# First layer of a four-layer image kernel: window rows in another order, copies of the inner rows, 25 rounds of products a group where there were 27

## What is computed

```python
def _denoise_block(x, w1, b1, w2, b2, w3, b3, a, b, c):
    trip = _triplets(x)             # channels t-1, t, t+1 (mirrored at the ends)
    xf = trip.reshape(B * T, C, H, W)
    o = a * _conv_reflect(xf, w1, b1, 1, 2) + b * _conv_reflect(xf, w2, b2, 2, 4) + c * _conv_reflect(xf, w3, b3, 4, 8)
    return jnp.tanh(o).reshape(B, T, H, W)
y = _denoise_block(x, blk1...)
z = _denoise_block(y, blk2...)
```

## Time and profile before

| | us |
|---|---|
| median of 3 runs | 5376.93 (5367.36 to 5379.23) |
| profiled execution, first to last instruction (the span) | 5383.9 |
| PE busy | 4994.9 (93% of the span) |
| DVE, ACT, POOL busy | 3365.2, 2396.6, 1362.4 |
| matmuls of the first layer's convolutions (L679) | 3027.2 busy, 55296 instructions |

### The profile page before, as it was taken

The page is one execution under the profiler, slowest core; times in us unless marked ns, Lnnn a source line. Parts: engine busy times, 40 slices in busy tenths (PEclk is TensorE's granted clock), DMA queues, the critical chain, the costliest instruction groups (busy, mean ns, idle before and its releaser), DMA issues. The chain is left out here.

```text
span 5383.9 us, 178367 instructions
## 1 busy us (share of the span) xinstructions
PE 4994.9 (93%) x78653; PEld 3092.8 (57%) x78653; DVE 3365.2 (63%) x6195; ACT 2396.6 (45%) x2999; POOL 1362.4 (25%) x1629
## 2 busy tenths in 40 slices
PE   4998999899899999999999997998777799999998
PEld 2444444444447569997666663443556466666665
DVE  5543444344342555555555546887999788888888
ACT  1222222222221111111111117885999689899997
POOL 0000000000001111111111100000777355555556
PEclk9999999999999999999999998999999999999999
DMA  8677777777666767667667657998688366666664
GB/s 246 217 228 235 224 228 232 223 223 237 222 209 199 226 200 239 207 203 236 203 208 236 205 178 277 321 325 302 256 308 309 129 152 152 150 150 153 151 152 120
DMA packets 366864, 1166.78 MB, mean 217 GB/s; under 512 B 60457, under 2 KB 61096, under 8 KB 287018
## 3 DMA queue, kind: packets, MB, share of 16 engines
q1 hardware_dynamic: 363928, 1152.98, 69.0%
q10 hardware_dynamic: 2162, 2.39, 0.2%
HBM read 683.58 MB, written 453.51 MB: 211 GB/s over the span
## 5 line engine op out<-in xcount | busy, mean ns | idle before, releaser
L679 PE MATMUL c_p<-c_w,wc 128*32 128x512 f16 x55296 | 3027.2, 381 | 91.1 <-DMA c_w<-xs 81.1
L679 PEld LDWEIGHTS c_p<-c_w,wc 128*32 128x32 f16 x55296 | 1896.0, 97 | 1194.4 <-DMA c_w<-xs 76.2
L739 ACT ACTIVATE c_t<-c_p,cbias,cscale 128x512 f32<-128x512 f32 x512 | 397.9, 777 | 2582.6 <-PE c_p L679 2582.6
L591 DVE TENSOR_SCALAR c_y<-c_t 128x512 f16<-128x512 f32 x256 | 109.2, 426 | 855.1 <-ACT c_t L739 854.1
L601 DVE TENSOR_TENSOR a_x<-c_t,a_x 128x512 f32<-128x512 f32 x256 | 221.3, 865 | 666.7 <-ACT c_t L739 658.5
L1699 PE MATMUL f_P<-f_qh,f_wt 64*64 64x512 f16 x4608 | 545.7, 378 | 1.8 <-DVE f_t L1595 1.8
L1699 PE MATMUL f_P<-f_hl,f_wt 64*64 64x512 f16 x4608 | 545.3, 379 | 0.0
L1860 POOL TENSOR_TENSOR f_y<-f_y,f_x 128x512 f32<-128x512 f32 x256 | 330.7, 1292 | 449.3 <-DVE f_hl L1574 443.2
L1595 DVE SCALAR_TENSOR_TENSOR f_t<-f_P,f_kk,f_ci 128x256 f32<-128x256 f32 x1024 | 423.4, 476 | 12.8 <-PE f_P L1699 7.6
L810 POOL COPY c_y<-c_y 128x16 f16<-128x16 f16 x512 | 85.6, 197 | 1360.7 <-DVE c_y L593 1360.7
L1459 POOL TENSOR_TENSOR e_hl<-e_g,e_hl 128x2048 f16<-128x2048 f32 x63 | 257.1, 4081 | 609.3 <-ACT e_hl L1409 609.3
(11 more groups left out here) (263 smaller groups left out, 5887.4 us busy)
## 6 DMA issues: line engine op xcount, KB each, us to landing
c_w<-xs SPq DMA_DIRECT2D x576, 264.0 KB, 5.6
c_w<-ys SPq DMA_DIRECT2D x576, 264.0 KB, 4.0
d_x<-x SPq DMA_DIRECT2D x128, 1024.0 KB, 7.6
x<-d_x SPq DMA_DIRECT2D x128, 1024.0 KB, 5.1
ys<-c_y SPq DMA_DIRECT2D x576, 132.0 KB
xs<-a_hl SPq DMA_DIRECT2D x70, 1056.0 KB, 9.8
a_x<-in_x SPq DMA_DIRECT2D x256, 256.0 KB, 6.8
a_x<-in_x SPq DMA_DIRECT2D x128, 512.0 KB, 5.2
```

The costliest lines, as they stand in the source:

```text
L679: t = p.matmul(pg[32 * j:32 * j + 32, :], wu[:, blk, wl, var, di, :], buf[:, bk, xl * PW + PAD + dx:xl * PW + PAD + dx + NW], start=(di == ...
L739: s.activation(tt_[n % 3][:, :], pp[:, n % 4, :], ACT.Tanh, bias=cbias[:, blk:blk + 1], scale=cscale[:, blk:blk + 1]).then_inc(c_act, 1)
```

## The change

The 32 rows of a window are put on the partitions in another order (`slot`): the 16 rows of the band first, then the 4 above and the 8 below, then the 4 farthest above. `load` follows it with four transfers for every two channels, of 32, 16, 8 and 8 partitions, where there were two of 32; the bytes are the same, and so are the 8448 bytes a partition. All semaphore counts of loads double.

Two small tensors with two buffers each are filled for every group by copies: `near` takes the high half of partitions 0 to 95 (the band's rows and 4 on each side; POOL, 96x2112 values) and, on partitions 96 to 127, the low half of partitions 64 to 95 (DVE, 32x2112); `twice` takes the low half of partitions 0 to 63 as it is (DVE, 64x2112) and, on partitions 64 to 127, the same shifted by 3 columns (ACT, 64x2052). With it the column offsets -2 and 1, and -1 and 2, are done by one product. `products` then has 15 rounds on the window for the offsets 0, -8, -4, 4, 8 as before, 4 of the low weights on the window, 4 on `near` and 2 on `twice`: 25.

The copies for group n + 1 stand on each of the three engines at the beginning of the loop's body for group n, ahead of the normalization steps, of the tables, of `halves`, `total` and `evict`. They wait for the loads of the group's unit and until group n - 1 is multiplied. PE waits for them inside the group, after 19 rounds (`near`) and after 23 (`twice`). POOL makes the weights for the six new products once, by 12 small copies ahead of the first group; the swapped copy of the weights grows from 432 to 576 KB a transfer and waits for them.

```diff
@@ -39,9 +39,8 @@
...
-        h8, s = ((1, 0), (0, 0), (1, 1), (0, 1))[row // 8 + 1]
-        v8 = row + 8 * h8 - 16 * s
-        return 8 * (2 * v8 + chan % 2) + 4 * s + 2 * h8 + chan // 2
+        place = row if 0 <= row < 16 else 16 + (row + 4 if -4 <= row < 0 else row - 12 if row >= 16 else row + 20)
+        return 4 * place + 2 * (chan % 2) + chan // 2
@@ -294,7 +293,9 @@
...
         h = sb(ctx, "a_hl", [128, 8, 2, PW], F16)
-        wc = [sb(ctx, f"wc{i}", [128, 2, 2, 3, 9, 32], F16) for i in range(2)]
+        wall = [sb(ctx, f"wc{i}", [128, 4608], F16) for i in range(2)]
+        wc = [w[:, 0:3456].rearrange("p (a b v d c) -> p a b v d c", a=2, b=2, v=3, d=9) for w in wall]
+        wn = [w[:, 3456:4608].rearrange("p (a v e c) -> p a v e c", a=2, v=3, e=6) for w in wall]
@@ -331,6 +332,8 @@
...
         win.append(sb(ctx, "c_w1", [128, 16, RW], F16))
+        near = [sb(ctx, f"c_n{i}", [128, 4, PW], F16) for i in range(2)]
+        twice = [sb(ctx, f"c_2{i}", [128, 4, PW], F16) for i in range(2)]
@@ -344,7 +347,8 @@
...
-        w_c, w_f, w_t, w_sel, w_hi = (sem("w_" + n) for n in ("c", "f", "t", "sel", "hi"))
+        w_c, w_f, w_t, w_sel, w_hi, w_wn = (sem("w_" + n) for n in ("c", "f", "t", "sel", "hi", "wn"))
+        c_nh, c_nl, c_2a, c_2b = (sem("c_" + n) for n in ("nh", "nl", "2a", "2b"))
@@ -378,7 +382,18 @@
...
-            return 128 * sum(1 + (place(r)[2] == 0) for r in range(u % 2, u + 1, 2) if r)
+            return 256 * sum(1 + (place(r)[2] == 0) for r in range(u % 2, u + 1, 2) if r)
+        def rows_in(e, n):
+            u, g = divmod(n, 4)
+            if u == 0:
+                e.wait_ge(c_l0[g // 2], 256)
+            elif g == 0:
+                e.wait_ge(c_ld[u % 2], n_win(u))
+            if n >= 2:
+                e.wait_ge(c_pe, n - 1)
+            return win[u % 2][:, 4 * g:4 * g + 4]
@@ -616,6 +631,11 @@
...
+                def copies(n):
+                    w = rows_in(v, n)
+                    v.tensor_copy(near[n % 2][96:128], w[64:96, :, PW:RW]).then_inc(c_nl, 1)
+                    v.tensor_copy(twice[n % 2][0:64], w[0:64, :, PW:RW]).then_inc(c_2a, 1)
@@ -629,10 +649,13 @@
...
                 v0(2), v1(2)
+                copies(0)
...
                         i, s = stage_of(u, g)
+                        if 4 * u + g + 1 < 8 * NU:
+                            copies(4 * u + g + 1)
@@ -664,22 +687,38 @@
...
                     if u == 0:
-                        p.wait_ge(c_l0[g // 2], 128)
+                        p.wait_ge(c_l0[g // 2], 256)
...
                         p.wait_ge(c_act, n - 3)
-                    for di, dx in enumerate(DX):
-                        for z, (wl, xl) in enumerate(((0, 0), (0, 1), (1, 0))):
-                            for j in range(4):
-                                bk = 4 * g + j
-                                var = 0 if (half, bk) == (0, 0) else (2 if (half, bk) == (1, 15) else 1)
-                                t = p.matmul(
-                                    pg[32 * j:32 * j + 32, :], wu[:, blk, wl, var, di, :],
-                                    buf[:, bk, xl * PW + PAD + dx:xl * PW + PAD + dx + NW],
-                                    start=(di == 0 and z == 0), stop=(di == 8 and z == 2), tile_position=(0, 32 * j))
+                    def four(weights, source, at, start=False, stop=False):
+                        for j in range(4):
+                            bk = 4 * g + j
+                            var = 0 if (half, bk) == (0, 0) else (2 if (half, bk) == (1, 15) else 1)
+                            t = p.matmul(pg[32 * j:32 * j + 32, :], weights[:, var], source[:, j, at:at + NW],
+                                         start=start, stop=stop, tile_position=(0, 32 * j))
+                        return t
+                    rows4 = buf[:, 4 * g:4 * g + 4]
+                    for di in (4, 0, 1, 7, 8):
+                        for wl, xl in ((0, 0), (0, 1), (1, 0)):
+                            four(wu[:, blk, wl, :, di], rows4, xl * PW + PAD + DX[di], start=(di, wl, xl) == (4, 0, 0))
+                    for di in (2, 3, 5, 6):
+                        four(wu[:, blk, 1, :, di], rows4, PAD + DX[di])
+                    if n == 0:
+                        p.wait_ge(w_wn, 12)
+                    p.wait_ge(c_nh, n + 1)
+                    p.wait_ge(c_nl, n + 1)
+                    for e, di in enumerate((2, 3, 5, 6)):
+                        four(wn[pr % 2][:, blk, :, e], near[n % 2], PAD + DX[di])
+                    p.wait_ge(c_2a, n + 1)
+                    p.wait_ge(c_2b, n + 1)
+                    four(wn[pr % 2][:, blk, :, 4], twice[n % 2], PAD - 2)
+                    t = four(wn[pr % 2][:, blk, :, 5], twice[n % 2], PAD - 1, stop=True)
@@ -739,6 +778,10 @@
...
+                def copies(n):
+                    w = rows_in(s, n)
+                    s.activation(twice[n % 2][64:128, :, PAD - 2:PAD - 1 + NW], w[0:64, :, PW + PAD + 1:PW + PAD + 2 + NW], ACT.Copy).then_inc(c_2b, 1)
@@ -794,11 +840,31 @@
...
+                def copies(n):
+                    w = rows_in(q, n)
+                    q.tensor_copy(near[n % 2][0:96], w[0:96, :, 0:PW]).then_inc(c_nh, 1)
+                def near_weights(blk):
+                    hi, to = wc[0][:, blk, 0], wn[0][:, blk]
+                    for z, (rows, of, e, d) in enumerate(((slice(0, 96), slice(0, 96), 0, 2), (slice(0, 96), slice(0, 96), 2, 5),
+                                                          (slice(96, 128), slice(64, 96), 0, 2), (slice(96, 128), slice(64, 96), 2, 5),
+                                                          (slice(0, 64), slice(0, 64), 4, 2), (slice(64, 128), slice(0, 64), 4, 5))):
+                        q.tensor_copy(to[rows, :, e:e + 2], hi[of, :, d:d + 2]).then_inc(w_wn, 1)
+                        q.wait_ge(w_wn, 6 * blk + z + 1)
...
                 mirror(1)
+                q.wait_ge(w_hi, 6)
+                near_weights(0)
+                near_weights(1)
+                copies(0)
...
                         i, s = stage_of(u, g)
+                        if 4 * u + g + 1 < 8 * NU:
+                            copies(4 * u + g + 1)
@@ -841,10 +907,10 @@
...
                     for gp in (0, 1) if p == 0 else (p + 1,):
-                        for h8 in range(2):
-                            e.dma_start(win[half][gp % 2 + 2 * h8:128:4, 4 * g:4 * g + 4].rearrange("p k w -> p (k w)"),
-                                        dram(src, pair(b, gp, 0, 16 * half + 4 * g) + h8 * (8 * VP - RW),
-                                             [[CP, 16], [RW, 2], [1, 4 * RW]])).then_inc(c_ld[half] if u else c_l0[g // 2], 16)
+                        at = pair(b, gp, 0, 16 * half + 4 * g)
+                        for first, off, n in ((0, 0, 32), (80, RW, 16), (64, 12 * VP - RW, 8), (112, 8 * VP - RW, 8)):
+                            e.dma_start(win[half][first + gp % 2:first + 2 * n:2, 4 * g:4 * g + 4].rearrange("p k w -> p (k w)"),
+                                        dram(src, at + off, [[CP, n], [1, 4 * RW]])).then_inc(c_ld[half] if u else c_l0[g // 2], 16)
@@ -895,9 +961,9 @@
...
                 load_x(3)
+                e.wait_ge(w_wn, 12)
                 for q in range(2):
-                    e.dma_start(wc[1][q:128:2].rearrange("p a b v d c -> p (a b v d c)"),
-                                wc[0][1 - q:128:2].rearrange("p a b v d c -> p (a b v d c)")).then_inc(w_sw, 16)
+                    e.dma_start(wall[1][q:128:2, :], wall[0][1 - q:128:2, :]).then_inc(w_sw, 16)
```

## The result

The changed kernel takes 5661.5 us (median of 4 runs, 5656.31 to 5665.76) where the kernel before, beside it on the same chip, takes 5378.1: a ratio of 1.0518, with a 95% interval of 1.0494 to 1.0542. The prediction said 5382, with a range of 5250 to 5520. It is wrong, and the range too.

A forecast was written before the change was run, and what follows sets the result against it. PE was taken to bound block two and pace block one, with four nearly full DMA engines close behind. Block two's -111 was given back by loads, start and image changes: total +5, 5389 less 7, 5382 us; range 5250 to 5520.

The forecast's parts named there:

- PE in block two: Block two: two rounds fewer, 0.432 us a group in 256 groups, -111 us if nothing else binds.
- entry and image changes: Block two: its entry was to cost +7 us and its three image changes +3 each, +9.
- Copies in block two: Block two: DVE's copies 0.70 us each, ACT's 1.9, POOL's 2.1, all fitting idle time; nothing on the path.
- Rival C: Block two: DVE and POOL get in each other's way, a group takes 6.6 us, +200 instead of -111, 5690 us; chance 0.09.
- Loads in block one: Block one: twice the loads, same bytes; 3.4 us more a pair, 6.9 at p = 0, on four nearly full DMA engines.
- The start: Start of block one: 64 loads instead of 32 ahead of the next input's transfers, +18 us (bounds 4 and 20).
- Four full engines get 8 rows more a pair: Block one: the four DMA engines carrying stores of ys get 8 more rows a pair, 3.4 us; at p = 0 16, 6.9 us.
- Copies in block one: Block one: DVE's copies stand ahead of `v0`, cutting a PE-paced pair's saving from 3.5 to 1.7 us; the weights' copies end early.
- PE's stall at `v0`: Block one: PE's wait for `v0` grows from 1.9 us by 1.4 and 0.43, to 3.7 us.
- rival B: Block one: SP's issue binds, each of 28 pairs 3 us worse, 5 us more at 7 image changes, 5500 us; chance 0.13.
- PE in block one: Block one: two rounds fewer would save 3.5 us a pair; only the last 4 pairs, paced by PE, gain: -7 us.
- A: Block one: PE paces it, not the loads, 32 x -1.7 = -54 us, 5230 us, or 5300 half realized; chance 0.28.

The follow-up runs named there:

- e2: The changed kernel with copies made for the first two groups only: 5439.3 us, ratio 1.0103.
- e8: The changed kernel with POOL's copy of the high half made for the first two groups only: 5450.0 us, ratio 1.0124.
- e15: e4 with the high half's copy done by ACT behind the eviction instead of by POOL: 5508.3 us, ratio 1.0234.
- e20: The change in block two alone, copies behind the other steps, POOL's done by ACT; block one as in the kernel before: 5300.6 us, ratio 0.9855.
- e1: The kernel before with the changed row order and four load transfers, 27 rounds and no copies: 5541.0 us, ratio 1.0296.
- e21: The kernel before with four load transfers of 32, 16, 8 and 8 partitions, each spread over all 128 partitions: 5449.5 us, ratio 1.0118.
- e5: The kernel before with each transfer of a window's load cut into two even ones of 16 partitions: 5402.8 us, ratio 1.0047.
- e3: The changed kernel with the row order and two load transfers of before, copies and 25 rounds kept: 5539.3 us, ratio 1.0296.
- e4: The changed kernel with DVE's copies moved behind normalization steps and tables, ACT's behind evict: 5622.2 us, ratio 1.0443.
- e13: The kernel before with the next input's transfers issued by ACT behind an eviction, not by SP: 5386.3 us, ratio 1.0006.
- e11: The kernel before with the changed loads and stores of ys as 16-partition transfers over all engines, half issued by ACT: 5729.1 us, ratio 1.0646.

## Why the prediction was wrong

By the terms of its sum, in us of the profiled execution:

- **PE in block two, -111.** Right: 3.5 us a pair in e2, e8, e15 and e20. With entry and image changes (+16 in the sum; 25 measured, from 112 less the 87 by which e2's block two is shorter) it leaves -87.
- **Copies in block two, nothing on the path.** This step failed, and by most: +161 us (1577 against e2's 1416). The prices of the copies were right: 0.70 us for DVE's, 1.92 for ACT's, and 2.3 for POOL's where 2.1 was taken. What was left out is that two of DVE's *new* operations wait while POOL's copy runs. Rival C had the mechanism, but named only L601 as held up and let DVE's one-input operations cover it, with a chance of 0.09. The two copies that the change itself adds to DVE are exposed as well. Its price was too high (a group of 6.6 us; 6.13 measured, 392.3 us for an image's 64 groups), as part of POOL's copy does run beside the reductions. The Trainium skill says this of exactly such copies (VectorE: DVE Perf Modes, mode 4×_2P, and SBUF — State Buffer, who interferes with whom): a 16-bit copy with one SBUF input uses both ports and so contends with POOL, and a tensor_reduce does not. The trace agrees on both: 1500 against 706 ns, 677 against 676.
- **Loads in block one.** In the sum +107 us with the start, the entry into block two and PE's gain at the end; alone, with 27 rounds, they cost 134 (e1), and with 25 rounds and no copies 139 (e2). The direction was right, the working only in part. The start, +18 in the sum, was right: e1's first eviction is 4.2 us late, but the one at 248.78 before stands at 266.24, and from there to 346.76 the delay is 17 to 20 us. "Four full engines get 8 rows more a pair" priced only the split, at 89 us (10, 58 and 21) where e21 less e5 has 44. The place of the transfers, 63 us, did not stand in it at all. That the term comes as near as it does is partly luck: one part was priced at twice its cost, another at nothing.
- **Copies in block one.** In the sum they cost nothing. Only PE's stall at `v0` was to grow, from 1.9 to 3.7 us, and that came nearly true: in the third image PE waits for it 3.3 us at most. But it was not the only stall. The copies cost +60 us on the changed loads (1941 against e2's 1881), +89 on the old ones (e3, against before). PE's waits for `v1` (L683) grew from 2.3 us to 154.9 and those for POOL's copy from none to 28.4 (of the 101.7 above; the rest is in block two), while e2's 262.8 us for windows fell to 47.4. That a copy waits for the next unit's windows while other steps stand behind it was named in rival B, as an aside, for `evict` and `halves` and without a price. Of the 60 us the order gives back 19 (e4), and leaving POOL's copy out 34 (e8); no run has both, so how the 60 divide stays open.
- **PE in block one.** The two rounds bring nothing while loads bind: 1875 in e1, 1881 in e2.

So in block one 133.7 us for the loads, 5.7 more with fewer rounds and 60.1 for the copies, in block two -87.4 by the rounds and 160.8 for the copies, and 3.6 behind them: the 276.5 us.

Of the rivals A is refuted (an image of 466 us, not under 415). B fails by its own sign: in the changed kernel SP still waits 50 us in all from 580 to 1045 us, and its issues average 0.78 us. Its count of issues is refuted by e5 and e13 besides; with 74 issues a pair, in e11, SP does bind. C happened, mildly. The range failed since its cases were taken as alternatives: block one's loss and block two's came together, and no case had both. My test for C, a group of block two over 5.5 us, was the right one: it is 6.13, and 5.40 in e2.

## To carry to other kernels

Before a copy is given to POOL because it is idle, list the DVE operations it will run beside, the new ones first: the 16-bit copies and the two-input operation waited for it here, 1.42 us a group beside a POOL copy of 2.3 us, and the one-input fp32 reductions did not. Count a cut-up DMA by three things: the number of issues, the split over engines, and the partitions each piece spans. Where copies wait for a transfer, they are better placed behind the steps that somebody else waits for (e4: 40 us in all), and where two stages have different limits, a change can be made in one of them alone: e20.

## What the runs showed that I had not expected

**The clock makes a wait dearer.** PE's timeline after waits, at the second image of the changed kernel (19 rounds are 76 matmuls):

```profile
580.31 4.27 PE L702 MATMUL c_p<-c_w,wc 128*32 128x512 f16 x76
...
603.61 6.62 PE L702 MATMUL c_p<-c_w,wc 128*32 128x512 f16 x76 [6.89 <-DMA c_w<-xs]
```

The same 76 matmuls take 4.27 us undisturbed and 6.62 after a wait of 6.89: another 2.35 us on top of it, at a granted clock of 1.00 from 580.31 to 584.41 and 0.63 from 603.61 to 610.05. From 1371.30 to 1378.00 us, behind PE's wait of 3.32 us for `v0`, the granted clock is 0.62, so most of it at 1.2 GHz, against 1.00 from 1361 to 1366:

```profile
1361.00:1366.00 5.00, 5.00 (x100) 2.49 (x96) 3.00 (x5) 2.71 (x2) 2.83 (x4) 1.00 0.74 212
1371.30:1378.00 6.70, 6.70 (x81) 2.74 (x84) 0.60 (x1) 0.00 (x0) 0.33 (x2) 0.62 0.62 186
```

Over the second image 64 groups at 5.40 us are 346 us, and PE is busy for 384.82 of the 465 from 580 to 1045. So about 39 us of an image are the clock, an estimate that agrees with its granted 0.90 there, and 80 are waits.

**More issues can be nearly free.** 16 more a pair cost block one 7.5 us in 32 pairs (e5), all of it at the start. The prediction had 9.6 us of SP's time a pair for them, against 9 us of room, and they took less: the even pieces land 3.8 us after their issue (5.6 in the earlier trace rows), and an issue of the input, held up for 1.55 us on average before, takes 1.26. SP's waits from 580 to 1045 us fall from 52.1 to 23.1 us: its queue absorbed the issues out of waits and hold-ups.
